# Twelve tiles' slots in place of eight for the rows gathered back at the end of the mixture stages

## What is computed

```python
def mixture(x, gate_w, w1, w2, w3, ws1, ws2, ws3):      # x: 4096 tokens x 256, after layernorm
    scores = softmax(x @ gate_w.T)                      # 16 experts
    # the best 2 of 4 groups of experts, then the best 4 experts of these
    weights, indices = top4(scores masked by group)
    c = zeros(T, 16); c[t, indices[t]] += weights[t]
    a = silu(einsum('td,edi->tei', x, w1)) * einsum('td,edi->tei', x, w3)   # i: 128
    y = einsum('tei,eid,te->td', a, w2, c)
    z = (silu(x @ ws1) * (x @ ws3)) @ ws2               # shared expert, 256 wide
    return y + z
x = x + 0.5 * mixture(layernorm(x), ...)
```

## Time and profile before

| | |
|---|---|
| median of three runs | 4177.82 us |
| the profiled execution | 4176.92 us, span 4175.0 us |
| granted TensorE clock, mean | 0.89 |
| busy share PE, DVE, ACT, POOL | 82%, 57%, 48%, 29% |
| end of stage f, from the first gather back | 3973.1 to 4175.0 us |

### The profile page before, as it was taken

How to read it: one execution, slowest core, us unless ns; L and a number is a source line. 1 busy time by engine, 2 the same in 40 slices (tenths; PEclk the granted TensorE clock), 3 DMA queues, 4 the chain that set the end, 5 groups by cost and what they waited for, 6 DMA issues and landing times. The chain is left out here.

```text
span 4175.0 us, 71302 instructions
## 1 busy us (share of the span) xinstructions
PE 3417.6 (82%) x23668; PEld 2585.4 (62%) x23669; DVE 2394.9 (57%) x4826; ACT 2006.2 (48%) x4064; POOL 1204.7 (29%) x1030
## 2 busy tenths in 40 slices
PE   4599948989896479992598799999999999539954
PEld 4499945555554469992498656566666656429943
DVE  4644445656664554435755565765676575485535
ACT  1566624444443166663444265655565565344411
POOL 2154321121110134432364021122022110226565
PEclk6699978999998579995699899999999999759976
DMA  3244220000002144325256300011011000415544
GB/s 125 92 97 101 36 63 6 17 17 27 17 16 85 54 128 87 81 36 146 80 166 179 133 26 19 14 31 32 2 32 32 17 16 6 136 57 166 160 152 129
DMA packets 209043, 294.07 MB, mean 70 GB/s; under 512 B 32992, under 2 KB 170208, under 8 KB 208480
## 3 DMA queue, kind: packets, MB, share of 16 engines
q1 hardware_dynamic: 155744, 176.32, 12.7%
q0 software_dynamic: 52992, 113.82, 11.8%
HBM read 193.20 MB, written 96.86 MB: 69 GB/s over the span
## 5 line engine op out<-in xcount | busy, mean ns | idle before, releaser
L2459 ACT ACTIVATE e_prob<-e_s_ps,e_small 128x512 f32<-128x512 f32 x512 | 346.5, 684 | 174.4 <-PE e_t_ps L2349 91.5
L2595 DVE TENSOR_REDUCE e_small<-e_s_ps 128x2 f32<-128x1024 f32 x256 | 313.0, 1223 | 143.7 <-PE e_s_ps L2336 135.4
L1867 ACT ACTIVATE b_pt<-b_t_ps 128x1024 f32<-128x1024 f32 (+3 forms) x256 | 180.7, 706 | 308.3 <-PE b_t_ps L1799 307.2
L2550 POOL TENSOR_TENSOR e_wide<-e_small,const 128x512 f32<-128x512 f32 x64 | 66.5, 1039 | 778.6 <-DVE e_small L2684 778.6
L2349 PE MATMUL e_t_ps<-const,e_prob 128*128 128x128 f32 x2048 | 270.6, 274 | 11.4 <-ACT e_pt L2448 6.1
L2370 PE MATMUL e_z_ps<-e_pt,e_v 128*64 128x512 f32 x1024 | 275.5, 617 | 0.4 <-DVE e_zf L2691 0.4
L2349 PEld LDWEIGHTS e_t_ps<-const,e_prob 128*128 128x128 f32 x2048 | 235.0, 141 | 59.1 <-issue 24.2
L2050 DVE TENSOR_REDUCE b_small<-b_s_ps 128x2 f32<-128x1024 f32 (+3 forms) x256 | 209.7, 819 | 85.0 <-PE b_s_ps L1778 80.9
L2601 DVE COPY e_pt<-e_t_ps 128x512 f32<-128x512 f32 x256 | 175.3, 685 | 68.2 <-PE e_t_ps L2349 64.4
L692 DVE TENSOR_TENSOR ce_h_lo<-ce_hid,ce_h_hi 128x512 fp32r<-128x512 f32 x128 | 88.6, 692 | 206.9 <-ACT ce_h_hi L639 185.3
L692 DVE TENSOR_TENSOR ae_h_lo<-ae_hid,ae_h_hi 128x512 fp32r<-128x512 f32 x128 | 88.7, 693 | 206.0 <-ACT ae_h_hi L639 184.0
(11 more groups left out here) (779 smaller groups left out, 11225.9 us busy)
## 6 DMA issues: line engine op xcount, KB each, us to landing
o_rows_dram<-d_big SPq DMA_DIRECT2D x36, 512.0 KB
o_rows_dram<-f_big SPq DMA_DIRECT2D x36, 512.0 KB
ae_raw<-w_dram SPq DMA_DIRECT2D x16, 1024.0 KB
ce_raw<-w_dram SPq DMA_DIRECT2D x16, 1024.0 KB
d_big<-x_dram SPq DMA_DIRECT2D x16, 512.0 KB, 9.2
f_big<-x_dram SPq DMA_DIRECT2D x16, 512.0 KB, 8.8
d_raw<-m_dram SPq DMA_DIRECT2D x54, 128.0 KB, 3.5
f_raw<-m_dram SPq DMA_DIRECT2D x54, 128.0 KB, 3.3
```

Source lines behind the costliest of these rows:

```text
L1867: act.activation(pt[:, kt % 2, a, :, 0:width], t_ps[:, :, 0:width], ACT.Exp).then_inc(p_ready, 1)
L2459: act.activation(prob[:, at], s_ps[:, at], ACT.Exp, bias=nmx[:, at:at + 1], accum_out=sums[:, buf, h * QT + s:h * QT + s + 1]).then_inc(p_ ...
L2595: dve.tensor_reduce(nmx[:, at:at + 2], s_ps[:, at:at + 2], AX.X, ALU.max, negate=True).then_inc(mx_ready, 1)
```

## The change

The number of slots, and with it the part of `w_hi` that they cover, the waits and the number of `taken` semaphores.

```diff
@@ -725,7 +725,7 @@
 TWO, TURN = 2, BODY // 2
 TILE_STEPS = COLS // TWO
 AHEAD = BODY
-RAW, TAKE, BY_POOL = 4, 8, 12
+RAW, TAKE, BY_POOL = 4, 12, 12
 
 CHUNKS = ((0, 2), (2, 5), (5, NG))
 LOGIT = 2 * E1
```

## The result

The changed kernel takes 4195.73 us (median of six runs, 4192.27 to 4200.85), the kernel before 4174.06 us beside it (six runs, 4166.92 to 4180.38). The ratio is 1.0053, with a 95% interval of 1.0043 to 1.0064: slower by about 22 us. The profiled execution has a span of 4197.0 us against 4175.0.

A forecast was written before the change was run, and what follows sets the result against it. Stage f was taken to be bound by unbroken gather runs that hold TensorE back until GpSimd pauses. Terms 20.3 - 2.3 = +18.0 us on 4176.9 gave 4194.9, forecast as 4195 us; range 4170 to 4208, likeliest case 4190 to 4200.

The forecast's parts named there:

- 16 gathers more in the first burst, 20.3 us: Stage f's first GpSimd burst: 48 gathers instead of 32, so it ends 20.3 us later, at 4033.9.
- The release 4.5 us after the burst, so nothing more: TensorE comes free 4.5 us after the first burst, at 4038.4 instead of 4018.07; lag bounds 2.4 and 6.2 us.
- The head start of TensorE, taken at nothing: TensorE's 30 instructions during the added 20.3 us count as nothing; if counted, they give 3.7 us back.
- Windows and bursts the same, only moved: After the first release, bursts 2 and 3 (36 gathers each), pauses, loads and stores move by 20.3 us, lengths unchanged.
- The last burst short, at most 2.3 us back: Stage f's end: 8 gathers left instead of 24, saving only VectorE's waits for gathers, at most 2.3 us.
- Rival A: TensorE's slow stretches are not the gathers' doing; only 2.3 us at the end are won: 4174.6 us, chance 0.17.
- Rival B: GpSimd is the bound and TensorE doesn't mind longer bursts; pauses go, 28.4 us less: 4148.5 us, chance 0.20.
- Rival C: The longer burst makes TensorE slow again sooner, adding a pause and half a stretch, 12 + 9 us: 4216 us, chance 0.07.
- only a pause releases TensorE: In stage f, a gather run lasting some 20 us holds TensorE back until GpSimd pauses; releases follow by 2.4 to 4.6 us.

The follow-up runs named there:

- e2: Changed kernel (twelve slots) with the 128 gathers of stage f and VectorE's waits for them left out; 4094.21 us.
- e1: Four slots instead of the changed kernel's twelve (eight before); 4171.97 us, ratio to the kernel before 0.9991.
- e7: Changed kernel, GpSimd zeroing 256 spare words after each stage f gather, pitch 1.61 us; 4197.63 us, ratio to the kernel before 1.0002.
- e8: Changed kernel, 256 spare words zeroed after each of stage f's first 80 gathers, routed rows taken two groups after own part; 4180.99 us, ratio to before 0.9968.
- e3: Changed kernel with stage f's gathers replaced by plain DMAs of the same bytes, issued by SP; 4107.39 us.
- e5: Changed kernel with the gathers of both mixture stages replaced by plain DMAs of the same bytes, issued by GpSimd; 4101.82 us.
- e4: Changed kernel, GpSimd zeroing 32 spare words after each stage f gather, pitch 1.37 us; 4169.20 us, ratio to the kernel before 0.9990.
- e11: As e8 (changed kernel, first 80 gathers paced, lead of two groups) but with 128 spare words; 4186.35 us, ratio to the kernel before 0.9989.

## Why the prediction was right

The forecast was 4195 us, and 4195.73 was measured. Its base was 4176.9 and the kernel before had 4174.06 beside the result, so the difference of 22 us is the fairer thing to hold against +18.0. That the total was met within 1 us is luck: a base 2.8 us too high and a change 3.7 us too small cancel.

- *16 gathers more in the first burst, 20.3 us.* 60.46 us for 48 against 40.47 for 32: 19.99 us.
- *The release 4.5 us after the burst, so nothing more.* This is the term that was too small. From the burst's end to the own part it took 6.99 us instead of 4.61, so 2.4 us came on top. Even my upper bound, 1.7 us more for 16 more gathers, was too small.
- *The head start of TensorE, taken at nothing.* I reckoned with 30 instructions in the added time; TensorE did 7 matmuls and 7 loads in 19 us, half of that. Nothing was the right value: counted from the first gathers, the own parts of groups 3, 5 and 7 come 23.9, 23.2 and 22.4 us later than in the kernel before, the first one 22.4.
- *Windows and bursts the same, only moved.* Nearly. The second window freed ten tiles, the next nine; group 3's own part came 25.3 us later, group 5's 24.5, group 7's 23.8.
- *The last burst short, at most 2.3 us back.* VectorE had no wait for a gather at the end and gave back 1.8 us between the last own part and the last mix. The last burst had 4 gathers, not 8, and with 40 and 36 gathers the two before it were not the 36 and 36 of the forecast.
- The rest, 1.3 us, is the first gather's later start, which the change has nothing to do with.

*Rival A* is out by e2, and e1, where the release came 20 us sooner. *Rival B*, GpSimd as the bound with TensorE unharmed, is what e7 and e8 bring about, but only with gathers further apart; at their own pace it does not happen (45.1, 67.5 and 67.6 us to the first own part). *Rival C* did not come in the first pair. The second stretch began 29 us after its burst.

What the forecast had only as a correlation, pauses of GpSimd and releases of TensorE, is now shown as a cause: without gathers (e2) and with plain DMAs (e3, e5) there are no slow stretches, with a shorter burst (e1) the first is shorter, with wider pitch (e7) it is gone. One sentence of the prediction is too strong, that only a pause releases TensorE: in e4 VectorE's second own part came at 4029.32 and in e11 the last at 4147.28, both in the middle of a burst. What in TensorE the gathers hold back isn't shown. The size is less firm than the sign: +0.53% in one set, +0.22%, about half of the forecast, in another.

## What to carry to other kernels

Look at what a wait protects before you remove it: here GpSimd's waits for a free slot were what let TensorE get on again after each slow stretch, and a deeper buffer let the producer hold back the engine that its own consumer waits for. A stall named "remote" or "issue" on an engine with nothing to wait for is best explained by laying other engines' bursts beside it, and a second place with the same code and a shorter burst (here stage d) is a free experiment. If indexed gathers share the time with a busy TensorE, slow them down where TensorE is needed and let them go where it isn't.

## What the runs showed of the hardware that was not expected

- Indexed gathers of GpSimd, 128 rows each, back to back at 1.26 us, bring TensorE from 73 matmuls in 17.5 us down to 7 in 19 us. Its starts are then 0.70, 1.40 or 2.10 us apart, in the longest stretch 2.80. Plain DMAs of the same size do not, from SP (127 matmuls in 27.4 us) or from GpSimd at 0.54 us each (147).
- Results that were long under way come free together: VectorE and ScalarE at 4018.21 and 4018.27 in the kernel before, 4041.92 and 4041.98 in the changed one, for matmuls that had started up to 48 us earlier. Whether the matmuls themselves are late or only the news of their end, no run shows.
- Bytes don't count: 512-byte rows did the same as 1 KB rows (67.9 us to the first own part, and 67.5).
- The pace counts: slow at 1.26 us, later and milder at 1.37, not at 1.61. A store that fills by the pace of the gathers and drains by one per about 1.6 us would fit this and the 2.4 to 7 us until TensorE is free; that such a store exists, and what it is, no run shows. Nor does any run show whether the recording of instructions, which every experiment here had, takes part in the hold.
- The granted clock in the slow stretches is 0.50 to 0.58, near the 1.2 GHz level, after TensorE had already become slow: in the kernel before it is still 1.00 from 3990.7 to 3992.5 and 0.99 to 3995.0, where TensorE starts 4 matmuls in 4.3 us after 35 in 5.7, and 0.50 from there on. In e7 and e2 it stays at 0.88 to 0.94 in the same place. It goes with the stall and does not explain it: at the low level the same matmuls take 0.43 us each, not 1.4.
